# Layer norm factor as exp(-0.5·ln(var+eps)) with one ScalarE function table, in a cross-attention kernel

## The reference

```python
def _layernorm(x, axis=-1, eps=1e-05):
    m = jnp.mean(x, axis=axis, keepdims=True)
    v = jnp.var(x, axis=axis, keepdims=True)
    return (x - m) / jnp.sqrt(v + eps)

x = x + _L0_xattn_ref(_layernorm(x), ctx_4096, ctx_4096, Wq, Wk, Wv, Wo)   # 32 heads of 16, 8 key/value heads
x = x + _L0_attn_ref(_layernorm(x), Wq, Wk, Wv, Wo)                        # causal, rotary, same heads
x = x + _L0_ffn_ref(_layernorm(x), weight_q3, weight_norm, bias)           # 3-bit weight, 512 to 512
```

## Time and profile before

| | before |
|---|---|
| median of 3 runs | 364.55 us (363.93, 364.55, 364.71) |
| the profiled execution | 363.73 us, of which 361.9 us from the first to the last instruction |
| instructions | 8398 |
| mean granted clock of TensorE | 0.986 of full speed |
| bytes moved | 41.25 MB, mean 114 GB/s |

### The profile page before, as it was taken

The page is one execution under the profiler, slowest core; times in us unless marked ns, Lnnn a source line. Parts: engine busy times, 40 slices in busy tenths (PEclk is TensorE's granted clock), DMA queues, the critical chain, the costliest instruction groups (busy, mean ns, idle before and its releaser), DMA issues.

```text
span 361.9 us, 8398 instructions
## 1 busy us (share of the span) xinstructions
PE 339.8 (94%) x2962; PEld 246.0 (68%) x2962; DVE 232.2 (64%) x420; ACT 203.2 (56%) x371; POOL 104.4 (29%) x195
## 2 busy tenths in 40 slices
PE   8999778999999999999999999998788989999996
PEld 4855546777777777777777777765366748875664
DVE  2977655766766766766757667657845237886652
ACT  4543226667757766676776677567656622275310
POOL 1432813133133133132241331330103141551410
PEclk9999898999999999999999999999998999999999
DMA  7970597575776486785876886979200000000002
GB/s 280 395 94 4 98 216 179 141 110 176 166 109 177 125 147 168 126 154 156 130 150 148 119 217 153 157 183 128 26 2 0 2 2 0 1 2 0 2 29 87
DMA packets 35820, 41.25 MB, mean 114 GB/s; under 512 B 15136, under 2 KB 30496, under 8 KB 33696
## 3 DMA queue, kind: packets, MB, share of 16 engines
q1 hardware_dynamic: 35360, 40.74, 52.5%
q10 hardware_dynamic: 432, 0.13, 0.1%
HBM read 24.07 MB, written 1.05 MB: 69 GB/s over the span
## 4 chain that ended last, share of the span: by engine, by line
PE 80%; DVE 7%; ACT 3%; DMA 2%; SPq 2%; issue 2%; POOL 2%; ACTq 0%; DVEq 0%; POOLq 0%
PE b_c L1089 8%; PE b_d L1030 8%; PE b_s L1051 7%; PE b_v L1005 4%; PE b_c L1234 4%; PE b_v L1007 4%; PE b_v L1006 4%; PE b_k L1007 4%; PE b_k L1005 4%; PE b_k L1006 4%; PE b_x L977 3%; PE b_t L977 3%; DMA kstack<-kparts 2%; PE b_c L1115 2%; PE b_c L1219 2%
## 5 line engine op out<-in xcount | busy, mean ns | idle before, releaser
L763 DVE TENSOR_REDUCE negmax<-b_s 128x1 f32<-128x512 f32 x128 | 87.9, 687 | 70.4 <-PE b_s L1051 63.2
L572 ACT ACTIVATE region<-b_c 128x512 f32<-128x512 f32 x128 | 74.6, 597 | 56.3 <-PE b_c L1089 33.5
L1051 PE MATMUL b_s<-kstack,qstack 96*128 96x512 bf16 x128 | 50.0, 390 | 9.0 <-DVE negmax L763 4.7
L1089 PE MATMUL b_c<-qstack,kstack 108*128 108x128 bf16 x512 | 51.3, 224 | 2.0 <-ACT region L572 1.5
L1089 PEld LDWEIGHTS b_c<-qstack,kstack 108*128 108x128 bf16 x512 | 33.1, 99 | 28.3 <-issue 21.4
L469 POOL TENSOR_TENSOR mwide<-negmax,zeros 128x4 bf16<-128x4 f32 x32 | 6.4, 200 | 122.4 <-DVE negmax L763 122.4
L1005 PE MATMUL b_v<-cT_h,wkv_h 128*128 128x512 f32 x64 | 31.7, 495 | 0.0
L1030 PE MATMUL b_d<-region,vaug 128*17 128x128 f32 x1024 | 31.4, 275 | 0.0
L1005 PE MATMUL b_k<-cT_h,wkv_h 128*128 128x512 f32 x64 | 30.8, 481 | 0.0
L460 POOL TENSOR_TENSOR kparts<-kres,zeros 128x512 bf16<-128x512 f32 x16 | 18.9, 1182 | 38.5 <-DVE kres L748 38.5
L1030 PEld LDWEIGHTS b_d<-region,vaug 128*17 128x17 f32 x1024 | 26.8, 98 | 2.0 <-issue 0.2
(11 more groups left out here) (397 smaller groups left out, 682.7 us busy)
## 6 DMA issues: line engine op xcount, KB each, us to landing
cx<-in_ctx_dram SPq DMA_DIRECT2D x16, 1024.0 KB, 5.1
kstack<-kparts SPq DMA_DIRECT2D x96, 128.0 KB, 4.3
qstack<-region SPq DMA_DIRECT2D x76, 32.0 KB, 2.9
xs<-in_x_dram SPq DMA_DIRECT2D x1, 1024.0 KB, 7.9
region<-in_L_xattn_Wq_dram SPq DMA_DIRECT2D x1, 1024.0 KB, 10.1
cx<-in_L_xattn_Wo_dram SPq DMA_DIRECT2D x8, 128.0 KB, 5.2
cx<-in_L_attn_Wq_dram SPq DMA_DIRECT2D x1, 1024.0 KB, 5.9
region<-in_L_attn_Wo_dram SPq DMA_DIRECT2D x8, 128.0 KB, 7.2
```

The source lines that it names most:

```text
L572: nc.scalar.activation(pT[:, g], b_c[g % 2][:].rearrange("p (a n) -> p a n", a=KT), ACT.Exp, scale=SCALE).then_inc(exp_ready, 1)
L763: nc.vector.tensor_reduce(negmax[:, n % 2, g:g + 1], b_s[:], AX, ALU.max, negate=True).then_inc(max_ready, 1)
L1051: nc.tensor.matmul(b_s[:], qstack[0:STACK, g, n % 4], kstack[0:STACK, n % 4, g], start=True, stop=True).then_inc(s_ready, 1)
L1089: last = nc.tensor.matmul(b_c[g % 2][:, P * a:P * a + P], kstack[0:ROWS, m % 4, g, P * a:P * a + P], qstack[0:ROWS, g, m % 4], start=True, ...
```

## The change

The factor 1/sqrt(var + eps) is computed as exp(-0.5 · ln(var + eps)). Both functions are taken from one table, `natural_log_exp_and_others`, which is loaded once at ScalarE's start by an instruction of its own; the copies and exponentials of the whole kernel use it too. The dummy Sqrt and its wait go. The adding of eps moves from VectorE into the bias of the Ln, a column `eps` that POOL fills at the start; the reciprocal on VectorE goes. ScalarE thus has two dependent small instructions in the place of one, and VectorE two fewer, in each of the eight tail instances, and the same in the opening. Semaphores are renamed to fit: ScalarE now waits for the mean and variance, VectorE for the finished factor.

```diff
+        eps = sb("eps_sb", [P, 1])
...
             nc.gpsimd.memset(zeros[:], 0.0).then_inc(zeros_ready, 1)
+            nc.gpsimd.memset(eps[:], EPS).then_inc(eps_ready, 1)
...
-            act.wait_ge(zeros_ready, 1)
-            nc.scalar.activation(rstd[:, 0:1], zeros[:, 0:1], ACT.Sqrt)
+            act.preload_act_table_set("natural_log_exp_and_others")
...
             def deviation(t, norm):
-                act.wait_ge(ln_var[norm], t + 1)
-                nc.scalar.activation(rstd[:, t:t + 1], mv[:, t, 1:2], ACT.Sqrt).then_inc(ln_std[norm], 1)
+                act.wait_ge(ln_aggr[norm], t + 1)
+                nc.scalar.activation(rstd[:, t:t + 1], mv[:, t, 1:2], ACT.Ln, bias=eps[:]).then_inc(ln_log[norm], 1)
+                act.wait_ge(ln_log[norm], t + 1)
+                nc.scalar.activation(rstd[:, t:t + 1], rstd[:, t:t + 1], ACT.Exp, scale=-0.5).then_inc(ln_rstd[norm], 1)
...
                 key_high(0, 0)
-                act.wait_ge(ln1_var, 1)
-                nc.scalar.activation(rstd[:], mv[:, :, 1], ACT.Sqrt).then_inc(ln1_std, 1)
+                act.wait_ge(eps_ready, 1)
+                act.wait_ge(ln1_aggr, TILES)
+                nc.scalar.activation(rstd[:], mv[:, :, 1], ACT.Ln, bias=eps[:]).then_inc(ln1_log, 1)
+                act.wait_ge(ln1_log, 1)
+                nc.scalar.activation(rstd[:], rstd[:], ACT.Exp, scale=-0.5).then_inc(ln1_rstd, 1)
...
-                    nc.vector.bn_aggr(mv[:, t], st[:, t]).then_inc(ln1_step, 1)
-                dve.wait_ge(ln1_step, 2 * TILES)
-                nc.vector.tensor_scalar(mv[:, :, 1], mv[:, :, 1], EPS, None, ALU.add).then_inc(ln1_var, 1)
-                dve.wait_ge(ln1_std, 1)
-                nc.vector.reciprocal(rstd[:], rstd[:]).then_inc(ln1_step, 1)
-                dve.wait_ge(ln1_step, 2 * TILES + 1)
+                    nc.vector.bn_aggr(mv[:, t], st[:, t]).then_inc(ln1_aggr, 1)
+                dve.wait_ge(ln1_rstd, 1)
...
                 nc.vector.bn_aggr(mv[:, t], st[:, t]).then_inc(ln_aggr[norm], 1)
-                dve.wait_ge(ln_aggr[norm], t + 1)
-                nc.vector.tensor_scalar(mv[:, t, 1:2], mv[:, t, 1:2], EPS, None, ALU.add).then_inc(ln_var[norm], 1)
 
             def normalise_rows(t, norm):
-                dve.wait_ge(ln_std[norm], t + 1)
+                dve.wait_ge(ln_rstd[norm], t + 1)
                 if t == 0 and norm == 0:
                     dve.wait_ge(qstack_loaded[(B - 1) % 4], 16 * SLOTS * (B // 4 - 1))
-                nc.vector.reciprocal(rstd[:, t:t + 1], rstd[:, t:t + 1]).then_inc(ln_rstd[norm], 1)
-                dve.wait_ge(ln_rstd[norm], t + 1)
```

More of the change, by code:

```diff
@@ L229, in perceiver @@
             m_transposed mrows_ready st_ready exp_ready pv_ready oraw_ready oraw_transposed rden_ready o_ready o_transposed oT_ready
-            ln1_step ln1_var ln1_std xh_ready xh_transposed xhT_ready q_summed q_high q_res q_mid q_low
-            wq_ordered zeros_ready mwide_ready unpack_step unpacked w_scaled w_step w_ready w_transposed wT_high wT_ready swq_high swq_ready swkv_high swkv_ready pv_zero weights_loaded swkv_loaded swq_loaded tail_weights_loaded
+            ln1_step ln1_aggr ln1_log ln1_rstd xh_ready xh_transposed xhT_ready q_summed q_high q_res q_mid q_low
+            wq_ordered zeros_ready eps_ready mwide_ready unpack_step unpacked w_scaled w_step w_ready w_transposed wT_high wT_ready swq_high swq_ready swkv_high swkv_ready pv_zero weights_loaded swkv_loaded swq_loaded tail_weights_loaded
             wo_summed x1_ready xn_transposed xnT_high xnT_ready
@@ L241, in perceiver @@
          m_transposed, mrows_ready, st_ready, exp_ready, pv_ready, oraw_ready, oraw_transposed, rden_ready, o_ready, o_transposed, oT_ready,
-         ln1_step, ln1_var, ln1_std, xh_ready, xh_transposed, xhT_ready, q_summed, q_high, q_res, q_mid, q_low,
-         wq_ordered, zeros_ready, mwide_ready, unpack_step, unpacked, w_scaled, w_step, w_ready, w_transposed, wT_high, wT_ready, swq_high, swq_ready, swkv_high, swkv_ready, pv_zero, weights_loaded, swkv_loaded, swq_loaded, tail_weights_loaded,
+         ln1_step, ln1_aggr, ln1_log, ln1_rstd, xh_ready, xh_transposed, xhT_ready, q_summed, q_high, q_res, q_mid, q_low,
+         wq_ordered, zeros_ready, eps_ready, mwide_ready, unpack_step, unpacked, w_scaled, w_step, w_ready, w_transposed, wT_high, wT_ready, swq_high, swq_ready, swkv_high, swkv_ready, pv_zero, weights_loaded, swkv_loaded, swq_loaded, tail_weights_loaded,
          wo_summed, x1_ready, xn_transposed, xnT_high, xnT_ready,
@@ L248, in perceiver @@
          ffn_summed, out_ready, out_stored) = (sems[name] for name in names.split())
-        ln_stats, ln_aggr, ln_var, ln_std, ln_rstd, xn_ready = (
-            [sem(f"{name}{i + 1}") for i in range(2)] for name in ("ln_stats", "ln_aggr", "ln_var", "ln_std", "ln_rstd", "xn_ready"))
+        ln_stats, ln_aggr, ln_log, ln_rstd, xn_ready = (
+            [sem(f"{name}{i + 1}") for i in range(2)] for name in ("ln_stats", "ln_aggr", "ln_log", "ln_rstd", "xn_ready"))
         ctx_loaded = [sem(f"ctx_loaded{i}") for i in range(2)]
```

## The result

| | before | after |
|---|---|---|
| median of four runs | 364.63 us (363.93 to 364.93) | 360.73 us (359.71 to 361.74) |
| the profiled execution | 363.73 us, span 361.9 | 360.37 us, span 358.5 |
| mean granted clock of it | 0.986 | 0.990 |

The ratio is 0.9896, with a 95% interval of 0.9863 to 0.9928. The forecast was 361.3 us. Two later measurements of the same two kernels gave less: 0.9947 (0.9917 to 0.9977) and 0.9938 (0.9908 to 0.9968). Why they differ, and what the change is really worth, is the subject of the experiments. The ratios here, and the means over many runs further on, leave out the few executions that a slower state of the chip had lengthened.

A forecast was written before the change was run, and what follows sets the result against it. TensorE, busy 94% of the span, was taken to bound the kernel. Gains of 0.1 + 1.28 + 1.7 + 0.15 = 3.2 us from the median 364.55 gave 361.3 us, range 360.4 to 362.8.

The forecast's parts named there:

- the clock falls all the same: Rival: TensorE's clock still falls after the remaining stalls near 273.9 us; gain 2.3 us, time 362.3 us; chance 0.25.
- chain at tile 0: First tail layer norm: Ln and Exp replace add, Sqrt and reciprocal; 0.05 to 0.15 us less, taken as 0.1.
- load at the first place: Load at 261.42, before line 572's exponential that TensorE's next product awaits: its full 1.28 us comes back.
- second place, without clock: Load at 271.81: VectorE limits the gain; line 1136 of tile 1 starts at 275.50 instead of 276.24, 0.74 us.
- second place, clock: From 276.24 to 278.60 TensorE stays at 2.4 GHz instead of 1.2, so 2.36 us take 1.18.
- tile 2: Tile 2's layer norm, which TensorE waited for: factor ready 0.14 to 0.24 us earlier, taken as 0.15.
- Which loads count: All ten later loads go; only those at 261.42 and 271.81, before line 572 behind a layer norm step, cost time.
- The rival by the Trainium skill's 2.66 us for a switch: A switch costs 1.28 us load plus 1.38 draining, so 2.66 gained at 261.42; sum 4.6 us, 359.9; chance 0.03.
- The sign that was to show the forecast: In the trace after, line 1136 of tile 1 about 2.1 us earlier than 276.24.
- POOL's wait: Second place: line 1017 would wait about 0.15 us for POOL's last part of the maxima, taken off the gain.
- TensorE's other work covers them: Tail copies of q and attention outputs, queued behind ScalarE's Ln and 0.2 us later each, cost nothing.
- What was added: POOL's eps fill and the opening's extra ScalarE instruction lie beside a busy TensorE and cost nothing.

The follow-up runs named there:

- before_two: The kernel before, unchanged, traced a second time: one execution, 359.69 us, tail stretch 100.20 us without a fall of the clock.
- load_first: Changed kernel with one table load put back before the exponential behind the first tile's transposed step in slot 15: 362.44 us, ratio 0.9975 to the kernel before.
- no_root: Kernel before with a plain copy in place of each Sqrt, which removes every table load but one: 362.64 us, ratio 0.9978 to the kernel before.
- again_two: Changed kernel, unchanged, measured a third time: 361.02 us, ratio 0.9938 to the kernel before; tail stretch 101.69 us.
- Copy_ahead: Changed kernel with the copy of the last batch's turned output (line 585) ahead of four query and key copies: 359.14 us, ratio 0.9873 to the kernel before.
- no_bias: Changed kernel with eps, the bias column, left out of the Ln: 361.81 us, ratio 0.9969 to the kernel before.
- again: Changed kernel, unchanged, measured once more: 361.22 us, ratio 0.9947 to the kernel before; tail stretch 98.59 us.

## Why the prediction was right or wrong

The time, 360.73 us, lay in the range, and faster was right. But the forecast of 3.2 us was a sum of terms of which two were wrong. At an even clock the change is worth 1.6 us in the tail, and 1.9 over all timed runs, nearer to the rival "the clock falls all the same" (2.3 us) than to the forecast. That the first measurement (3.9 us between the medians) bore the forecast out so well was luck: it drew a high median for the kernel before.

| term | forecast | found (before_two against after) |
|---|---|---|
| chain at tile 0 | 0.1 | 0.06 |
| load at the first place | 1.28 | 1.41 |
| second place, without clock | 0.74, less 0.15 for POOL | 0.40, less 0.16 |
| second place, clock | 1.18 | none shown |
| tile 2 | 0.15 | 0.14, less 0.28 |
| behind it | 0 | 0.05 |
| sum | 3.2 (3.3 before rounding the second place) | 1.62 |

*Which loads count.* Right: of the ten, the one at 261.42 and in part the one at 271.81, though that one only together with VectorE's two instructions. That seven of the tail's loads are free was right too.

*The first place.* The mechanism was right, with TensorE's work going on at once and nothing else late. The size was 0.13 short, for the overlap of two activations and the gaps around the load. The rival by the Trainium skill's 2.66 us for a switch ("ScalarE: Activation LUTs", What ACT_TABLE_LOAD costs) fell: load_first shows 1.41 for everything that the load adds, and no_root 1.42 for the loads that changed the set. The measurement decides.

*The second place.* The step that failed is the baseline. I took tile 1's transpose at 276.24 and called the tile late by 0.37 us of VectorE's work and 0.37 of the rest. But tile 1 was ready at 275.84, and TensorE reached it later because it ran at 1.2 GHz. VectorE's row in before, then VectorE's and TensorE's in before_two, where the clock was full:

```profile
275.29 0.55 DVE L889 TENSOR_SCALAR region<-xs,mv,rstd 128x512 f32<-128x512 f32 x1
```

```profile
272.62 0.55 DVE L889 TENSOR_SCALAR region<-xs,mv,rstd 128x512 f32<-128x512 f32 x1
...
273.22 0.66 PE L1136 MATMUL b_s<-ident_sb,region 128*128 128x128 f32 x4
```

There TensorE starts 0.05 us after the tile is done. So all there was to gain is VectorE's 0.37, and 0.40 was measured. The sign that was to show the forecast, tile 1 transposed about 2.1 us earlier, came true all the same (19.01 against 16.81, 2.20), but 0.33 of it is the low clock of before's trace (19.01 against 18.68). POOL's wait came as worked out: line 1015 starts 0.40 us after the product before it, in before_two 0.22.

*The clock.* This term failed as well. From one fall behind two stalls I concluded that with smaller stalls there would be none. The rows of again_two show falls behind what is left, and before_two none behind the full stalls. What the one trace could say was what a fall costs, not how often it comes. A small part of the term stays open: fewer falls may give up to 0.4 us, by the mean clocks above.

*Tile 2.* The chain gained 0.14 of the 0.15. But "TensorE's other work covers them", said of the copies behind the new pair, was wrong for one: with line 1134 earlier and the copies later, the products for the residual of tile 3 wait longer for line 585. That took 0.28 us, more than the chain had given. Copy_ahead shows the cause.

*What was added* at the start, the opening's pair and the renamed waits cost nothing that can be seen. The opening itself is not settled better than to the 2.7 us by which the start of the stretch spreads in before alone; that goes for the load at 58.80 too.

## What to carry to other kernels

Here a table load cost what TensorE waited for it and nothing else, so look for the one load that stands between a late copy and the product that needs the next exponential; here one of ten held nearly all. A single trace in which the clock fell gives false lateness downstream: check whether the engine that seems to wait was merely slow before it puts a term in the sum. And when a shared queue gets one more instruction, follow each thing queued behind it to whoever waits for it, since that is where the new stall came from.

## What the runs showed of the hardware

- Two activations that follow each other directly overlap by 0.1 us (copy at 260.33 for 0.60 us, exponential at 260.83); a table load between them takes its 1.28 us, that overlap and 0.03 of gaps, 1.41 together (load_first).
- An activation of one column takes 0.20 us for Sqrt (before), Ln (no_bias) and Exp (after) alike; a bias given as a column adds 0.09. The Exp starts 0.03 us after the end of the Ln that it waits for.
- The changed kernel, with the same stalls, had no fall of TensorE's clock (after, again) or two (again_two) in a stretch of 98 us, the kernel before none or one; a fall cost 1.35 to 1.70 us.
- A short stall in a matmul's row understates what it costs by the overlap that is lost: 0.23 us in the row, about 0.5 when it was removed.
